# Staged preparation, rotated rows apart from the sine products, masks kept once, and shifted rows in the norms' own buffers, in a recurrent, local-attention, global-attention and expert kernel

## The reference

```
xn = layernorm(x)
s  = recurrent(xn)                 # projection to 3 x 256, gates, scan over the tokens, projection to 128
g  = silu(local_network(xn))       # two layers, below
x  = x + s * g
xn = layernorm(x)
s  = global_attention(xn)          # 16 heads, key size 16, value size 64, softmax over the queries' axis
g  = silu(experts(xn))             # 8 experts, for 512 tokens (the batch the kernel takes last); others: bias alone
x  = x + s * g

local layer:
h = shift_token(x)                 # channels 64..127 come from the token before
q, k, v = split(h @ wqkv)          # 8 heads of 64
q, k = rotary(l2norm(q) * qs), rotary(l2norm(k) * ks)
x = x + local_attention(q, k, v) @ wo     # windows of 64, each sees itself and the one before
h = shift_token(x)
h = layernorm(h) * lg + lb
a, g = split(h @ w1 + b1)
x = x + (a * gelu(g)) @ w2 + b2
```

## Time and profile before

| what | us |
|---|---|
| three runs, median (lowest to highest) | 3417.7 (3413.98 to 3424.05) |
| the profiled execution, its own time | 3421.56 |
| its span, first to last instruction | 3419.8 |
| granted PE clock, mean over the span | 0.957 of full speed |

### The profile page before, as it was taken

How to read it: one execution, slowest core, us unless ns; L and a number is a source line. 1 busy time by engine, 2 the same in 40 slices (tenths; PEclk the granted TensorE clock), 3 DMA queues, 4 the chain that set the end, 5 groups by cost and what they waited for, 6 DMA issues and landing times.

```text
span 3419.8 us, 55040 instructions
## 1 busy us (share of the span) xinstructions
PE 2955.3 (86%) x20144; PEld 1430.4 (42%) x20144; DVE 2472.0 (72%) x4573; ACT 2549.2 (75%) x5722; POOL 871.9 (25%) x653
## 2 busy tenths in 40 slices
PE   4778789899888989888888988989898898998797
PEld 2345334444444434443444444444453443443243
DVE  3756777787777877777787778777777777786634
ACT  2566677787778778787778878777777877786666
POOL 0322213132231323223222313322231322221100
PEclk9899999999999999999999999999999999999899
DMA  2000101010010111011010100101010110101210
GB/s 80 4 1 1 47 27 52 26 46 28 18 52 28 49 30 52 18 35 42 23 47 30 52 26 29 41 23 52 25 52 26 39 35 15 52 23 52 87 52 22
DMA packets 113448, 122.78 MB, mean 36 GB/s; under 512 B 13426, under 2 KB 86684, under 8 KB 113180
## 3 DMA queue, kind: packets, MB, share of 16 engines
q1 hardware_dynamic: 113180, 119.26, 10.9%
HBM read 64.70 MB, written 54.53 MB: 35 GB/s over the span
## 4 chain that ended last, share of the span: by engine, by line
PE 59%; DVE 18%; ACT 14%; issue 5%; POOL 2%; SPq 1%; DMA 0%; DVEq 0%; ACTq 0%; POOLq 0%
PE pb L625 24%; PE o_bank L625 13%; PE e L625 9%; PE s L625 7%; DVE nmax L1367 3%; ACT ex L1085 3%; PE e L718 2%; PE pb L747 2%; DVE stat L1260 2%; PE pb L777 1%; DVE scratch L1303 1%; ACT scratch L981 1%; POOL scratch L1468 1%; DVE scratch L1267 1%; ACT side L954 1%
## 5 line engine op out<-in xcount | busy, mean ns | idle before, releaser
L1367 DVE TENSOR_REDUCE nmax<-s 128x1 f32<-128x512 f32 x1024 | 678.4, 684 | 225.9 <-PE s L625 223.9
L1085 ACT ACTIVATE ex<-s,nmax 128x512 f32<-128x512 f32 x1024 | 697.4, 684 | 169.1 <-DVE nmax L1367 136.3
L625 PE MATMUL o_bank<-ex,vsc 128*64 128x512 f32 x2048 | 518.4, 629 | 8.6 <-POOL vsc L1493 7.0
L1463 POOL TENSOR_TENSOR scratch<-scratch 128x1024 f32<-128x1024 f32 x128 | 302.9, 2367 | 696.2 <-DVE scratch L1272 696.2
L625 PE MATMUL s<-qs,ks 96*128 96x512 bf16 x1024 | 385.0, 398 | 99.6 <-ACT ex L1085 94.1
L625 PE MATMUL e<-wqkv,hsh 128*128 128x512 f32 x768 | 428.8, 640 | 42.7 <-ACT scratch L981 28.3
L1493 POOL TENSOR_TENSOR vsc<-vrow,rinv 128x256 f32<-128x256 f32 x256 | 156.7, 614 | 1180.0 <-DVE rinv L1378 1111.6
L1468 POOL TENSOR_TENSOR scratch<-scratch,stat 128x1024 f32<-128x1024 f32 x128 | 243.7, 1904 | 444.8 <-DVE stat L1284 444.8
L1015 ACT ACTIVATE scratch<-pb,stat 128x128 f32<-128x128 f32 x1024 | 290.7, 374 | 23.9 <-DVE stat L1291 23.4
L625 PE MATMUL pb<-cent,w 128*128 128x512 f32 (+1 forms) x384 | 237.3, 703 | 55.1 <-ACT mlp_h L1042 24.7
L981 ACT ACTIVATE scratch<-e 128x512 f32<-128x512 f32 x256 | 152.2, 594 | 137.3 <-PE e L625 124.9
(11 more groups left out here) (217 smaller groups left out, 5641.7 us busy)
## 6 DMA issues: line engine op xcount, KB each, us to landing
parts_store<-side SPq DMA_DIRECT2D x64, 384.0 KB, 2.6
qs<-parts_store SPq DMA_DIRECT2D x128, 192.0 KB, 2.7
ks<-parts_store SPq DMA_DIRECT2D x128, 192.0 KB, 3.3
parts_store<-side SPq DMA_DIRECT2D x64, 256.0 KB, 2.9
parts_store<-side SPq DMA_DIRECT2D x64, 128.0 KB, 2.7
xin<-in_L_attn_x SPq DMA_DIRECT2D x16, 256.0 KB, 3.6
out<-o1T SPq DMA_DIRECT2D x16, 256.0 KB, 3.9
wqkv<-in_L_ffn_wqkv SPq DMA_DIRECT2D x1, 1536.0 KB
```

The lines of the kernel that those rows point to most:

```text
L625: return pe.matmul(o, l, r, start=start, stop=stop, skip_group_check=True)
L1085: A(ex[:, w % 2, j, :], s_bank[c % 2][:], ACT.Exp, bias=nmax[:, c % 8:c % 8 + 1], accum_out=rsum[:, w % 2, j:j + 1]).then_inc(GA, 1)
L1367: V.tensor_reduce(nmax[:, c % 8:c % 8 + 1], s_bank[c % 2][:], X, ALU.max, negate=True).then_inc(GV, 1)
L1463: G.tensor_tensor(l_q, l_c, l_q, ALU.add).then_inc(f.sem["pool"], 1)
```

## The change

- **Loads in groups.** The x of batch 0 is loaded right behind the constants. The other loads stand in six groups with a semaphore each, in this order: `wqkv` of layer 0; tables and masks; the networks' weights with `wqkv` of layer 1; recurrent weights; global weights. `wqkv` and the tables are two loads each now. Each first user waits for its group.
- **Preparation as a flow.** `setup` has steps with marks like the others and a lane w in the phase "first". On PE, `qk` and `bias 0` come directly behind the first norm's products, before the second x and the first projection; `bias 1`, `v` and `o` come later. It uses the banks `s_bank`.
- **Rotation.** The sine products go to a buffer `l_s` of their own; the wait for `tk` of the previous tile moves to POOL, before the sum.
- **Masks** are kept once each and read with a repeated index.
- **Shift.** `mlp_in` is gone: the shifted rows go to the norm's buffer for the squares, `mlp_h[:, 1]` or `sq`, and a memset on DVE clears their first column each time. The first layer's shift waits for `y` of the second layer's network two batches before; the second layer's for nothing new.
- **Order.** All strings of `ORDER` are new.

```diff
+def setup_steps():
+    return [("masks",), ("tab", 0), ("qk",), ("bias", 0), ("bias", 1), ("gates",), ("tab", 1), ("v", 0), ("v", 1), ("o", 0), ("o", 1)]
...
     "first": {
-        "pe": ("4s2psps3ps3pspqpsqsprpqpqprp2rqpqpq3r4pspsrqp2qprprq2rspsqpsprp2rp2rqprps2prp2rqrp2rpqrqrq2rpqrpqrpr"
+        "pe": ("3s2wsps2pspw2p3s3pspwpq2pqwpr2pq2prq2rpq2pq2p2rpsrqrs3q2r2pqsrsprqpsrprqrprp2rspqprprqrpq2rp2r2p2rq2"
...
     "middle": {
-        "dve": ("p2v2gsgsg2pgv3g2s2pvgpq2g2s2p2gps2gqrv2s2grsvpsp2gspgrqvpg2r2g2sgprsgsrvgsqrs2gpspr2gvrgspsprgspsrvq"
-                "2p3spvsrq2g2pgrgprgrsgsv2gsps2gsvsrgr2gsvr2g2s2grv2g2rsgqgvrgrs2grs2gvq2g3r2g3r2gr"),
-        "pool": ("2vpv2pv2p2vs3p2vpv2pvp2s2pv2ps2vs3v"),
+        "dve": ("pvgsv2gs2p2gv2g2sg2pgpvs2gqs2g3pgvsqgr2sgrsv2ps2grgpsgqprgrv2g2spgrsgvrs2gsqsrg2psrgvgrsrg2psgspsvqp"
+                "s2pr3svr2gq2pr2gprgrg2sv2gspsvg2sr2gr2gsvr2g2s2grvr2grgsqgrgvrgrgs2gvqr2g2r2g3rs2gr"),
+        "pool": ("2vpv2pv2p2vps2p2vpv2pvpspspv2ps2vs3v"),
...
-        masks = sb("masks", [P, 2, 4, P], BF16)
+        masks = sb("masks", [P, 2, P], BF16)
...
-        mlp_in, sq, cent, rstd, cent0 = (sb(n, [P, N]) for n in ("mlp_in", "sq", "cent", "rstd", "cent0"))
+        sq, cent, rstd, cent0 = (sb(n, [P, N]) for n in ("sq", "cent", "rstd", "cent0"))
...
-        l_qk, l_c, l_q = (sc(1024 * i, 1024) for i in range(3))
+        l_qk, l_c, l_s, l_q = (sc(1024 * i, 1024) for i in range(4))
...
-            for dst, src in LOADS:
-                sp.dma_start(dst, src).then_inc(loaded, 16)
+            sp.dma_start(const[:], a["const"][:, 0:3 * P]).then_inc(loaded["const"], 16)
...
-            for i in range(-1, B + 3):
+            load_x(0)
+            for group, dst, src in LOADS:
+                sp.dma_start(dst, src).then_inc(loaded[group], 16)
+            for i in range(0, B + 3):
                 step(i)
...
+            pe.wait_ge(cleared, 1)
+            pe.wait_ge(loaded["const"], LOADED["const"])
+
+            def setup_does(b, s):
+                kind, SE = s[0], setup.sem["pe"]
+                if kind == "qk":
+                    pe.wait_ge(loaded["global"], LOADED["global"])
+                    for r in range(2):
+                        pe.transpose(s_bank[0][:, P * r:P * r + P], raw_q[:, r, :], ident)
+                        last = pe.transpose(s_bank[0][:, P * (2 + r):P * (2 + r) + P], raw_k[:, r, :], ident)
+                elif kind == "bias":
+                    l = s[1]
+                    if l:
+                        need(pe, setup, "dve", b, ("bias", 0), "b")
+                    else:
+                        pe.wait_ge(loaded["network"], LOADED["network"])
...
-                        mm(banks[par], identb[:], masks[:, 0 if t == 0 else 1, :, :].rearrange("p h n -> p (h n)"), stop=False)
+                        mm(banks[par], identb[:], masks[:, min(t, 1), :].unsqueeze(1).broadcast_to([P, PAIRS, P]), stop=False)
...
-                    norm(f, b, s, x3s[b % 2] if s[1] == "out" else mlp_in[:])
+                    norm(f, b, s, x3s[b % 2] if s[1] == "out" else (norm1 if l else norm0)[1])
...
-                    o = l_q.rearrange("p (k h d) -> p k h d", k=2, d=DH)
-                    if t:
-                        need(dve, f, "pe", b, ("tk", t - 1), "t")
+                    o = l_s.rearrange("p (k h d) -> p k h d", k=2, d=DH)
...
                     if l == 0:
-                        need(dve, post[1], "pe", b - 2, ("centre", 1), "c")
-                    elif b < B - 1:
-                        need(dve, post[0], "pe", b + 1, ("centre", 0), "c")
-                    else:
-                        need(dve, post[1], "pe", b - 1, ("centre", 1), "c")
+                        need(dve, post[1], "pe", b - 2, ("y",), "y")
+                    mlp_in = (norm1 if l else norm0)[1]
+                    V.memset(mlp_in[64:P, 0:1], 0.0)
                     V.tensor_copy(mlp_in[0:64, :], xl[0:64, :])
...
-                    G.tensor_tensor(l_q, l_c, l_q, ALU.add).then_inc(f.sem["pool"], 1)
+                    if t:
+                        need(pool, f, "pe", b, ("tk", t - 1), "t")
+                    G.tensor_tensor(l_q, l_c, l_s, ALU.add).then_inc(f.sem["pool"], 1)
```

More of the change, by code:

```diff
@@ L235 @@
 }
+SETUP_MARKS = {
+    "masks": {"dve": ["m"]},
+    "tab": {"dve": ["t"]},
+    "qk": {"pe": ["t"], "dve": ["c"]},
+    "bias": {"pe": ["b"], "dve": ["b"]},
+    "gates": {"dve": ["n", "d", "g"], "act": ["e", "l", "f"]},
+    "v": {"pe": ["t"], "act": ["c"]},
+    "o": {"pe": ["t"], "act": ["c"]},
+}
 STEPS = {
+    "setup": setup_steps(),
     "pre": [("x",), *norm_steps("in")],
@@ L280, in lanes @@
     out = {k: [(flow, n + shift, s) for n in turns for flow, shift, s in v if 0 <= n + shift < B] for k, v in parts.items()}
+    if phase == "first":
+        out["w"] = [("setup", 0, s) for s in STEPS["setup"]]
     if phase == "last":
@@ L393, in build @@
         attn, post = (flows["attn0"], flows["attn1"]), (flows["post0"], flows["post1"])
-        loaded, routing_loaded = sem("weights_loaded"), sem("routing_loaded")
+        loaded = {n: sem(f"{n}_loaded") for n in ("const", "wqkv", "tables", "network", "gru", "global")}
+        routing_loaded = sem("routing_loaded")
         x_loaded, out_stored = sem("x_loaded"), sem("out_stored")
@@ L688, in gru_does @@
                         need(pe, pre, "dve", 1, ("normed", "in"), "n")
+                if j == k == b == 0:
+                    pe.wait_ge(loaded["gru"], LOADED["gru"])
                 mm(bank_d, gru_w1[:, k * DIN + P * j:k * DIN + P * j + P], xn0[b % 2]).then_inc(gru.sem["pe"], 1)
@@ L705, in qkv_does @@
                         need(pe, f, "dve", b, ("shift",), "h")
+                        if l == b == 0:
+                            pe.wait_ge(loaded["wqkv"], LOADED["wqkv"])
                     n = ("q", "k", "v").index(kind)
@@ L781, in head_does @@
                     need(pe, f, "act", b, ("oturn", t), "t")
+                    if l == b == t == 0:
+                        pe.wait_ge(loaded["network"], LOADED["network"])
                     for r in range(PAIRS):
@@ L805, in post_does @@
                         need(pe, f, *(("dve", b, ("a", j - 1), "a") if j else ("act", b, ("g", JM - 1), "g")))
+                    if kind == "g" and b == j == 0:
+                        need(pe, setup, "dve", 0, ("bias", l), "b")
                     at = HID * (kind == "g") + P * j
@@ L1163, in _ @@
[L1163 to L1168 removed]
+            dve.wait_ge(cleared, 1)
+            H = DH // 2
@@ L1230, in gru_does @@
                 elif kind == "g5":
+                    if b == 0:
+                        need(dve, setup, "dve", 0, ("gates",), "g")
                     need(dve, gru, "act", b, ("g4", j), "g")
```

307 lines of the change are left out of this document (172 added, 135 removed).

## The result

The changed kernel takes 3380.69 us (median of 4 runs, 3379.11 to 3382.44), against 3415.84 for the kernel before beside it: a ratio of 0.988, 95% interval 0.9861 to 0.9899. Its profiled execution took 3379.99 us, with a span of 3378.2. The forecast was 3383, range 3346 to 3403. The number came out; most of the terms that it was summed from did not, and the experiments are about that.

What follows compares the result with a forecast made beforehand. No engine is full, so the order in which each takes its steps decides. Terms -19.7 + 3 - 5 - 10 - 3 = -34.7 give 3386.9 from 3421.6; less 3.9 to the median: 3383 us, range 3346 to 3403.

Steps and rivals of the forecast that it cites:

- Start (-19.7): Kernel's beginning: first projection with wqkv at 33.2 us instead of 52.92, held by the last load group, -19.7 us.
- Deferred preparation (+3): Filling phase: preparation steps moved between other steps, half of PE's 5.7 us counted, +3 us.
- sine products (-5): Filling phase: DVE's wait for transposes moves into POOL's idle time, a third of 13.7 us gained, -5 us.
- Square buffers (0): Shifted rows in the norm's square buffer: the removed wait worth nothing by itself; memsets at worst 3 us.
- Masks (0) and memsets: Repeated mask reads cost 0, casts fall in load time; 32 memsets at 0.10 us each, at worst 3 us.
- The turns (-0.8 each): Twelve middle turns: earlier third rotation and later global residual on DVE shorten the norm's wait, -0.8 a turn, -10 us.
- Last phase (-3): Kernel's end: new order, but no resource of the global layer and experts changed, -3 us, ends +6 and -7.
- (a): Rival, turns: second slow-clock stretch goes from eight turns at 2.7 us, 22 us more gained, 3361 us; chance 0.22.
- (b): Rival, turns: POOL's queue delays scaled values, a slow stretch and wait more each turn, 3461 us; chance 0.04.
- (c): Rival, start: only the start pays, and less, with deferred steps on the path, 3411 us; chance 0.12.
- slower rival: Same as (b): POOL's late values give each turn one more slow-clock stretch and a wait, 3461 us; chance 0.04.

Runs made afterwards that it cites:

- e11: Kernel before with only the staged start and the masks kept once, old orders and buffers: 3416.81 us, ratio 0.998 to the kernel before.
- e14: Changed kernel with the first x loaded behind all groups of weights, orders and buffers as changed: 3375.99 us.
- e4: Changed kernel with the second x loaded right behind the tables and q, k and biases prepared behind the first five projections: 3374.29 us.
- e5: Changed kernel with the old last-phase order, second x behind the tables, biases ahead of q and k, these behind the third transposes: 3352.27 us.
- e10: Changed kernel with the old last-phase order, second x behind the tables, q, k and biases prepared behind the first five projections: 3353.65 us.
- e9: Changed kernel with DVE's third rotation back behind the gate products and the global residual ahead of the recurrent sums, in the middle turns: 3366.43 us.
- e13: Changed kernel with its last weight loaded in two halves, orders and buffers as changed: 3377.89 us.

## Why the prediction was right, and where it was not

The sum was right because its errors cancelled, which is luck. In the table's parts the forecast and the trace stand so: up to turn 3, -33.0 us measured where start, deferred preparation and sine wait summed to -21.7; twelve turns, -30.5 (2.5 a turn) where -10 was forecast; from batch 15's copy to the end, +21.9 where -3 was. -33.0 - 30.5 + 21.9 = -41.6, the difference of the spans, against -34.7. (Cut at the global projections, as in rows 1, the twelve turns gain 20.6 and the rest loses 17.1; the last of those twelve already holds steps of the last phase.)

*Start (-19.7).* The place was right: the last load holds PE's fourth step, and the first product came at 34.4, forecast 33.2. The landing was mis-sized: the group was issued by 25.8 and landed at 30.5, 4.7 us later, not 1.9; the 1.9 was that of a load of 1 KB, and this one has 512 KB. What failed is the next step, that this gain goes to the end of its own. In the old order of that phase 18.1 us of lead become 2.4 (e11); in the new one 9.4 us of lag become 10.2 (e14), and a further lead of 16 leaves 4 to 8 (e4, e5, e10).

*Deferred preparation (+3), sine products (-5).* The wait moved to POOL and fell into its idle time, as told. With the old order, taking it off DVE is worth 2.8 by turn 3, of which 0.5 us are PE's time without a matmul, so the -5 isn't shown. The missing term is the order of the first phase: I gave it a share of the sine wait only, and it is worth 18.7, of which 11.0 are waits. The queues of the filling phase were not read step by step as those of the turn were. The preparation was put at 5.7 us of PE and half of it counted; in e11 PE's busy time up to turn 3 grows by 11.8, the lower clock included.

*Square buffers (0).* DVE showed no idle time before the copy in the turn, so I took the wait for worthless. By turn 3 the kernel with the buffers is 7.5 ahead with the old order, but DVE doesn't stand idle in front of the copy there either (neither before nor in e11), and only 1.5 us of it are PE's time without a matmul. So the reading of the wait holds; that the clock was higher is not explained. In the turns the buffers gain nothing.

*Masks (0) and memsets.* Right: 385 ns, and 59 ns each, 1.9 us over the kernel.

*The turns (-0.8 each).* The sign and the cause, the order, were right, the size 2.5, and the steps named were not the ones: with both set back a turn still takes 194.4. The hole is still there (4.13 to 4.50 us busy of 8 in each of the twelve turns, in the stretch 20 to 28 us behind the projection). A turn lost its waits for POOL's rows and for the probabilities and gained one for ACT's copies, none of which the prediction priced.

*Last phase (-3).* This is the step with the wrong sign. That no resource which fills it is changed was true and beside the point. From the twelfth projection to the end PE is without a matmul for 101.5 us where the kernel before has 95.3, which is the new order's, and PE is busy for 15.9 us more (589.45 against 573.54, 3218 matmuls against 3208) at a clock of 0.91 instead of 0.94. The second, larger part is the mechanism of the prediction's slower rival (more slow stretches), in the phase where it had not been looked for, and without POOL: PE waits for POOL's scaled rows for 6.1 us in all.

*Rivals.* (a) did not come: the second slow stretch of a turn is still there, now in all twelve. (b) did not come. (c) had the start paying and nothing else; with the old orders even the start leaves only 2.4 us at turn 3, and the orders of the first phase and of the turns are what pays.

The Trainium skill ("TensorE: Matmul & The Clock Gate", section "HAM oscillation — how this bites in real kernels") says that waits inside a loop throttle the array anew in every round. Nine of the twelve turns of the changed kernel agree (0.64 to 0.67 behind the hole); in three, with the same hole, the trace differs (1.00), and the measurement decides.

Open: what decides whether the clock falls behind a hole. A later first x (e14) or two moved steps in the turns (e9) went with the faster last phase in their traced execution and a higher mean clock in all their runs (0.957 to 0.958), and in e13 one run of five was the faster with nothing changed. Setting back one engine's order alone wasn't tried: the strings fit only each other, and two engines would each wait for a step behind the other's wait. Nor was the sine wait on DVE with the new orders, in which the sine product stands ahead of steps that the previous tile's transposes need; by that the buffer is what makes these orders possible, which no run shows. The masks (768 bf16 columns fewer) and the shared buffer of the shifted rows (512 f32) help to pay for its 1024 f32 columns.

## What to carry to other kernels

Read a phase's slack before a gain upstream of it is counted: 18 us at the start were worth 2 at turn 3 behind one order; behind the other a lag of 9 was paid in full, and of a further lead of 16 half or less was left. Where an order is written out for several phases, time each phase's order against the old one by itself, behind the phase that it will follow; here the orders of the first phase and of the turns carried the gain, and dropping that of the last phase gave a kernel that is 24 us faster than the change. And split each stretch into PE's busy time and its time without a matmul before a cause is named: where matmul time grows while the waits stay, read the granted clock before looking for a late producer.

## What the runs showed that was not expected

The same hole does not always cost the clock. In the changed kernel it fell behind nine of twelve equal holes; e14, with the same orders, agreed with it for ten turns and then took the eleventh and twelfth the other way round. Each of these two programs repeats itself (mean clock 0.949 to 0.952 in the four runs of the one, 0.957 to 0.958 in the four of the other), but e13 does not: over its five runs the mean clock went from 0.951 to 0.961 and the time from 3381 to 3360, so a hundredth of mean clock went with 21 us. A change of 10 us in this kernel can be such a turn of the clock, and only the stretches of the trace, not the total, tell the two apart.
